# Attention scores of four heads as one group of twelve matmuls, and the side work of each unit placed anew over three fixed banks

## What is computed

```
Xp = X Wp[h] + bp        (512 x 32 for each of 8 heads)
Xc = Xp C[h]^T
S  = Xc Xp^T             (512 x 512)
attn = tanh(A * S)
out = relu(attn Xp)
```

## Time and profile before

| | before |
|---|---|
| runs (3), us | 2223.23, 2228.31, 2232.1 |
| median, us | 2228.31 |
| span of the profiled execution, us | 2229.1 |
| instructions | 38475 |
| busy: PE, PEld | 2052.3 (92%), 1499.7 (67%) |
| busy: DVE, ACT, POOL | 1538.2 (69%), 1246.9 (56%), 1062.8 (48%) |

### The profile page before, as it was taken

How to read it: one execution, slowest core, us unless ns; L and a number is a source line. 1 busy time by engine, 2 the same in 40 slices (tenths; PEclk the granted TensorE clock), 3 DMA queues, 4 the chain that set the end, 5 groups by cost and what they waited for, 6 DMA issues and landing times. The chain is left out here.

```text
span 2229.1 us, 38475 instructions
## 1 busy us (share of the span) xinstructions
PE 2052.3 (92%) x12194; PEld 1499.7 (67%) x12194; DVE 1538.2 (69%) x3332; ACT 1246.9 (56%) x1870; POOL 1062.8 (48%) x1266
## 2 busy tenths in 40 slices
PE   7999999956999999967999999999999789999986
PEld 6988888845888888853454544444444478888853
DVE  6777777744666666654687778887876557767759
ACT  4444444414666666645766766675666257767630
POOL 3355555552333333326345565464642447777740
PEclk9999999977999999987999999998998899999998
DMA  7344445125555555643122211223221055556559
GB/s 288 146 170 172 171 171 181 39 82 172 167 184 175 176 183 172 179 152 132 57 95 83 98 62 62 77 82 103 74 67 32 6 181 182 187 167 191 187 204 350
DMA packets 138148, 315.42 MB, mean 142 GB/s; under 512 B 36990, under 2 KB 67808, under 8 KB 133952
## 3 DMA queue, kind: packets, MB, share of 16 engines
q1 hardware_dynamic: 106560, 271.77, 36.3%
q0 software_dynamic: 31488, 42.39, 5.5%
HBM read 206.67 MB, written 151.56 MB: 161 GB/s over the span
## 5 line engine op out<-in xcount | busy, mean ns | idle before, releaser
L1712 ACT ACTIVATE c_att<-c_att 128x1024 f32<-128x1024 f32 x256 | 270.0, 1057 | 210.5 <-DVE c_att L1914 208.3
L1914 DVE TENSOR_TENSOR c_att<-c_p_s,adj 128x1024 f32<-128x1024 f32 x256 | 301.1, 1216 | 86.5 <-PE c_p_o L1421 74.4
L2241 POOL DMA_INDIRECT moe_y<-d_y,d_goal x256 | 257.0, 1004 | 115.9 <-ACT d_y L2206 51.5
L995 POOL DMA_INDIRECT moe_y<-b_y,b_goal x144 | 155.4, 1079 | 327.8 <-DVE b_y L1047 293.9
L1408 PEld LDWEIGHTS c_p_s<-c_xcth,c_xpth 32*128 32x128 f32 x512 | 48.0, 185 | 208.3 <-issue 121.2
L154 PE MATMUL b_p_y<-b_w2h,b_hh 128*128 128x256 f32 x576 | 169.2, 294 | 7.4 <-DVE b_hl L160 4.0
L476 POOL DMA_INDIRECT moe_in<-a_xn,a_rows x128 | 141.5, 1106 | 57.6 <-issue 29.2
L160 DVE TENSOR_TENSOR b_hl<-b_ht,b_hh 128x512 fp32r<-128x512 f32 (+1 forms) x160 | 101.5, 638 | 88.8 <-ACT b_ht L1153 88.8
L155 PE MATMUL b_p_y<-b_w2l,b_hh 128*128 128x256 f32 x576 | 160.7, 279 | 0.0
L156 PE MATMUL b_p_y<-b_w2h,b_hl 128*128 128x256 f32 x576 | 160.6, 279 | 0.0
L1364 POOL DMA_INDIRECT moe_in<-c_xn,c_rows x128 | 130.6, 1020 | 53.8 <-issue 39.4
(11 more groups left out here) (273 smaller groups left out, 6147.4 us busy)
## 6 DMA issues: line engine op xcount, KB each, us to landing
b_w<-in_moe_w SPq DMA_DIRECT2D x80, 512.0 KB, 4.3
moe_in<-b_zeros SPq DMA_DIRECT2D x65, 520.0 KB, 10.8
d_xin<-moe_in SPq DMA_DIRECT2D x64, 520.0 KB, 3.5
adj<-in_adj SPq DMA_DIRECT2D x32, 1024.0 KB, 5.6
b_xin<-moe_in SPq DMA_DIRECT2D x32, 520.0 KB, 5.9
c_g<-moe_y SPq DMA_DIRECT2D x32, 512.0 KB
moe_y<-c_zeros SPq DMA_DIRECT2D x32, 512.0 KB
d_w<-in_moe_w SPq DMA_DIRECT2D x64, 256.0 KB
```

What stands on the lines that cost most here:

```text
L995: pool.indirect_dma_start(out=m["moe0_y"], out_offset=bass.IndirectOffsetOnAxis(ap=goal[:, h, t:t + 1], axis=0), in_=y[:, h, t, :], in_off ...
L1712: act.activation(part, part, ACT.Tanh).then_inc(att_ready, 1)
L1914: dve.tensor_tensor(att[:, u % 2, 2 * c:2 * c + 2, :], p_s[:, 2 * c:2 * c + 2, :], adj[:, h, u % T, :].unsqueeze(1).broadcast_to([P, 2, N] ...
L2241: pool.indirect_dma_start(out=m["moe1_y"], out_offset=bass.IndirectOffsetOnAxis(ap=goal[:, h, t:t + 1], axis=0), in_=y[:, h, t, :], in_off ...
```

## The change

The halves of a unit's scores are merged: `scores` now issues twelve matmuls, for each of the three operand pairs four heads one after the other, and raises `s_done` once for a unit. PE waits until both products of the unit before are done. `side_a(u)` is almost empty, and the order of a unit on PE is scores(u), `side_a(u)`, values(u - 1), `side_b(u)`. PE's loop no longer reaches into the next graph: the first scores of a graph are made in its own unit 0. DVE waits once for a unit's scores, before its first product.

The three banks of `p_w` no longer swap: LEFT, RIGHT and COUNT are 0, 1 and 2, and every piece of side work has one of them. Pieces are moved: the second half of the product with C and the last transpose back of a graph now stand in its own units 0 and 1 instead of the units 5 to 7 of the graph before; `apply1` moves from unit 0 to unit 7 of the graph before; the second half of the projection is cut in two (`only`); `down` moves half a unit to a unit later; on POOL `add_moe0` goes ahead of `scale3`, and `scale1` between the two halves of the scatter. ACT runs both tanhs of a unit first and all side work behind them. The number of matmuls, activations and DVE instructions of a graph stays the same, but that the second half of the projection is issued in two calls.

The core of the diff. In PE's `side_a` and `side_b` and in DVE's `side` the removed lines, which can be read in the kernel above, are left out, and ACT's side work, which follows PE's (each bank is emptied in the unit in which PE fills it), is left out whole:

```diff
                     weigh_moe0(b + 2)
+                    add_moe0(b + 2)
                 if not is_at(b, 0):
                     scale3(b - 1)
-                if more:
-                    add_moe0(b + 2)
-                if not (isinstance(b, int) and b < 2):
+                if b > 1:
                     scatter(q - 1, h, b - 2, 0)
-                    scatter(q - 1, h, b - 2, 1)
                 if more:
                     scale1(b + 2)
+                if b > 1:
+                    scatter(q - 1, h, b - 2, 1)
...
-            def scores(b, par, u, c):
+            def scores(par, u):

                 f, t = u // T, u % T
                 s, tok = of(f, par), slice(t * P, (t + 1) * P)
                 for n, (left, right) in enumerate(((xpth, xcth), (xpth, xctl), (xptl, xcth))):
-                    for i in (2 * c, 2 * c + 1):
+                    for i in range(HG):
                         r = slice(DH * i, DH * i + DH)
                         mm = pe.matmul(p_s[:, i, :], left[r, s, tok], right[r, f, :], start=(n == 0), stop=(n == 2))
                 mm.then_inc(s_done, 1)
...
-            def wide(w, f, src, bank, done, last_of=False):
-
-                for k in range(KD):
+            def wide(w, f, src, bank, done, last_of=False, only=range(KD)):
+
+                for k in only:
                     mm = pe.matmul(p_s[:, bank, :] if last_of else p_w[:, bank, :], w[:, k, f * P:(f + 1) * P], src[:, k, :],
                                    start=(k == 0), stop=(k == KD - 1))
-                mm.then_inc(done, 1)
+                if KD - 1 in only:
+                    mm.then_inc(done, 1)
...
                def side_a(u):
+                    if u == 4 and not last:
+                        wide(wp, 1, xt, LEFT, xpt_done, only=(1,))
+                def side_b(u):
+                    if u == 0:
+                        if going_down:
+                            wide(ws3, 1, xt3, RIGHT, up_done)
+                        elif late:
+                            keep_busy(RIGHT)
+                        if late:
+                            pe.wait_ge(member_ready, b - 1)
+                            if going_down:
+                                pe.wait_ge(hs_ready, KHS * (b - 2) + 1)
+                            else:
+                                pe.wait_ge(xp_ready, GRP * b + 1)
+                            count_before(pe, m, count, member, count_done)
+                        pe.wait_ge(xpt_ready, GRP * b + 2)
+                        pe.wait_ge(xpt_lo, GRP * b + 2)
                         if going_down:
                             pe.wait_ge(sh_ready, KHS * (b - 2) + 2)
+                        elif late:
+                            pe.wait_ge(sg_ready, b - 1)
+                        project_c(h, 1, LEFT)
+                    if u == 1:
+                        if post:
+                            pe.wait_ge(ot_ready, GRP * b)
+                            if late:
+                                pe.wait_ge(r2_step, R2 * (b - 2) + 2)
+                            else:
+                                pe.wait_ge(xp_ready, GRP * b + 1)
+                            turn_back(ot[:, 1], COUNT, back_done)
+                        if going_down:
+                            pe.wait_ge(hs_ready, KHS * (b - 2) + 2)
+                            down(0, RIGHT)
+                        elif late:
+                            keep_busy(RIGHT)
+                        pe.wait_ge(xct_lo, GRP * b + 2)
+                        turn_back(xpf[:, 1], LEFT, xp_done)
+                    if u == 2:
+                        if not last:
+                            pe.wait_ge(xn_ready, b + 2)
+                            if post:
+                                pe.wait_ge(x3_ready, GRP * b)
+                            else:
+                                pe.wait_ge(xp_ready, GRP * b + 1)
+                            turn(xn, 0, COUNT, tr_done)
                             pe.wait_ge(xp_ready, GRP * b + 2)
+                            turn(xn, 1, LEFT, tr_done)
                         if going_down:
                             pe.wait_ge(x4_ready, TB * (b - 2) + 1)
+                            down(1, RIGHT)
+                    if u == 3 and not last:
+                        pe.wait_ge(xt_ready, KD * (b + 2))
+                        wide(wp, 0, xt, COUNT, xpt_done)
+                        wide(wp, 1, xt, LEFT, xpt_done, only=(0,))
+                    if u == 4:
                         if post:
+                            pe.wait_ge(xn3_ready, b)
+                            if going_down:
+                                pe.wait_ge(x4_ready, TB * (b - 1))
+                            turn(xn3[:, 1 - h], 0, RIGHT, tr3_done)
+                            if not last:
+                                pe.wait_ge(xpt_ready, GRP * (b + 1) + 1)
+                            else:
+                                pe.wait_ge(x3_ready, GRP * b)
+                            turn(xn3[:, 1 - h], 1, COUNT, tr3_done)
+                    if u == 5:
+                        pe.wait_ge(ot_ready, GRP * b + 1)
+                        if post:
+                            pe.wait_ge(xt3_ready, KD * (b - 1) + 1)
+                        turn_back(ot[:, 0], RIGHT, back_done)
+                        if not last:
+                            pe.wait_ge(xpt_ready, GRP * (b + 1) + 1)
+                            if post:
+                                pe.wait_ge(xt3_ready, KD * b)
+                            turn_back(xpf[:, 0], COUNT, xp_done)
                         if post:
                             pe.wait_ge(xt3_ready, KD * b)
+                            if not last:
+                                pe.wait_ge(xpt_ready, GRP * (b + 1) + 2)
+                            else:
+                                pe.wait_ge(xp_ready, GRP * b + 2)
+                            logits(xt3, LEFT)
+                    if u == 6:
                         if not last:
+                            pe.wait_ge(x3_ready, GRP * b + 1)
+                            pe.wait_ge(xpt_lo, GRP * (b + 1) + 1)
+                            project_c(1 - h, 0, RIGHT)
                         if going_up:
+                            pe.wait_ge(sg_ready, b)
+                            wide(ws1, 0, xt3, LEFT, up_done)
+                            pe.wait_ge(xp_ready, GRP * (b + 1) + 1)
+                            wide(ws3, 0, xt3, COUNT, up_done, only=(0,))
                         elif post:
                             pe.wait_ge(sg_ready, b)
+                            keep_busy(LEFT)
+                    if u == 7:
+                        if going_up:
+                            wide(ws3, 0, xt3, COUNT, up_done, only=(1,))
+                            pe.wait_ge(sh_ready, KHS * (b - 1) + 1)
+                            wide(ws1, 1, xt3, LEFT, up_done)
+                        elif post:
+                            keep_busy(LEFT)
+                            keep_busy(LEFT)
                 for u in range(UNITS):
-                    for c in range(2):
-                        pe.wait_ge(prod_ready, 2 * (UNITS * b + u) + c + 1)
-                        if u + 1 < UNITS:
-                            if u + 1 == T and c == 0:
-                                pe.wait_ge(xct_lo, GRP * b + 2)
-                            scores(b, h, u + 1, c)
-                        elif not last:
-                            scores(b + 1, 1 - h, 0, c)
-                        if c == 0:
-                            side_a(u)
-                            if u > 0:
-                                values(b, h, u - 1)
-                            elif post:
-                                values(b - 1, 1 - h, UNITS - 1)
-                        else:
-                            side_b(u)
+                    if post or u > 0:
+                        pe.wait_ge(prod_ready, 2 * (UNITS * b + u))
+                    if u % T == 0:
+                        pe.wait_ge(xct_lo, GRP * b + u // T + 1)
+                    scores(h, u)
+                    side_a(u)
+                    if u > 0:
+                        values(b, h, u - 1)
+                    elif post:
+                        values(b - 1, 1 - h, UNITS - 1)
+                    side_b(u)
...
             def products(b, h, u, c):
                 n = UNITS * b + u
-                if c == 0 and not (isinstance(n, int) and n < 2):
-                    dve.wait_ge(av_done, n - 1)
-                dve.wait_ge(s_done, 2 * n + c + 1)
+                if c == 0:
+                    if n > 1:
+                        dve.wait_ge(av_done, n - 1)
+                    dve.wait_ge(s_done, n + 1)
...
                 def side(u):
                     if u == 0:
                         if going_down:
+                            gate_shared(b - 2, 1, p_w[:, RIGHT, :])
                         if late:
                             places_of(b - 2)
+                        if not post:
```

(21 more changed lines are left out.)

240 lines of the change are left out of this document (59 added, 181 removed).

## The result

The changed kernel takes **2106.42 us** (median of four, 2106.05 to 2108.89); the kernel before took 2230.20 beside it. The ratio is **0.9447 [0.9423, 0.9471]**: 5.5% faster. The direction was forecast and the size was not: 124 us less instead of 80, and the time lies under the range's low end of 2118.

What follows compares the result with a forecast made beforehand. PE was taken to bound the kernel, busy 92% of the span. Savings of 38 us (graphs 2 to 8), 23 (10 to 14) and smaller terms made 80, from 2229.1 to 2149, median 2148; range 2118 to 2182.

Steps and rivals of the forecast that it cites:

- the group at 0.89 us: PE's twelve merged score matmuls of a unit run all side by side in 0.89 us, saving 7.1 us a graph.
- Rival 1: Four row strips on PE share more: 1.1 us a group, 2160 (chance 0.14), or 1.6, 2195 (chance 0.06).
- the replay: Unit-by-unit sum of PE's and DVE's work in the attention stage: 40.6 us for graphs 2 to 8, 36.7 for 10 to 14.
- New unit 3: the 4.16 of the old unit 2 less 0.60, 3.56: DVE's side work in unit 3, taken from old durations: 3.56 us, beside 2.26 for the products.
- small gaps that the replay has not; I add them: 0.8 us beyond PE's busy time added to each graph's sum, giving 41.4 and 37.5 us.
- Half-clock stretches are kept as they are.: The time PE runs at half clock in the stage was assumed unchanged.
- rival 3: PE's clock falls at gaps in late graphs: single falls 2174 (chance 0.11), a lasting one 2298 (chance 0.05).
- The small terms of the sum: Savings estimated outside the main graphs: graph 9 5 us, graphs 1, 15 and 0 6, 4 and 2, ahead of graph 0 2.
- Rival 2: DVE stands idle during every unit's scores: 1.7 us saved in seven graphs, nothing later, 2216 us; chance 0.07.
- under 35: Sign of a right forecast: DVE's waits for PE in the stage shrink from 74 us to under 35.
- Rival 4: The twelve score matmuls run one by one on PE and nothing is left of the gain; no chance of its own given.
- POOL's "thin" slack: POOL's moved steps cost nothing: about 33 us of work under 41 a graph, some 2 us to spare at scale3.

Runs made afterwards that it cites:

- e11_before_add_early: The kernel before with only POOL's add_moe0 moved ahead of scale3: 2219.31 us, ratio 0.9970.
- e6_before_busy5: The kernel before with one more keep_busy in unit 5 of graphs 9 to 15: 2221.50 us, ratio 0.9966.
- e4_merge_only: The kernel before with its scores merged and everything else in its old place: 2287.61 us, ratio 1.0242.
- e9_pool_adds: The changed kernel with nine more 128x256 additions on POOL per graph from 2 on, ahead of the scatter: ratio 0.9568 to the kernel before, on another chip.
- e1_two_by_two: The changed kernel with a unit's twelve score matmuls issued as two groups of six, still one hand-over to DVE: 2107.66 us, ratio 0.9437.

## Why the prediction was wrong in size, step by step

**Right: the group at 0.89 us.** It took 0.90, with 0.34 and 0.23 between passes, as two strips took 0.89. Rival 1 is out at both its prices, and so is what stood beside it by the Trainium skill, "TensorE: Matmul & The Clock Gate", section "Measured speedup vs the span model": at 3.07x a group would take 1.1. (In rival 1, "39.6 to 40" for the late graphs does not follow from its own rule, which gives 40.0 - 1.4 = 38.6; its 2195 is off by some 6 us.) Of the argument one sentence was false: "No row shows four row strips at once". The score rows at 1023.39 do; I had read only graph 3's, and the doubt with rival 1's 0.20 was not needed.

**Right: the replay as a method.** Its units against those of graph 5 after:

| unit | 0 | 1 | 2 | 3 | 4 | 5 | 6 | 7 |
|---|---|---|---|---|---|---|---|---|
| forecast | 5.0 | 6.13 | 4.25 | 5.82 | 4.80 | 4.1 | 5.6 | 4.94 |
| measured | 4.49 | 6.11 | 4.25 | 4.11 | 4.71 | 4.31 | 5.40 | 5.17 |

Units 1 and 2 hit to 0.02 us, 4, 5, 6 and 7 to 0.25. The forecast was 40.6 without small gaps; the units measured sum to 38.5, and unit 3 alone makes 1.7 of the difference. That is also what the two experiments with the merge say: a unit is as long as the longer of PE and DVE in it. Which of the two holds a unit came out otherwise, though. The replay gave five of eight to DVE; in graph 4 PE is busy throughout in six, all but 2 and 5, and in units 1, 4 and 7 DVE lies 0.3 us or less behind it.

**Wrong, the first step: "New unit 3: the 4.16 of the old unit 2 less 0.60, 3.56."** The duration came from a stretch in which POOL's adds blocked half of the operations, and the change moves those adds away: `add_moe0` was looked at for what waits for it, and priced at "nothing". Freed of it, the piece takes 1.4 us and unit 3 is PE's, at 4.11. That is 7 x 1.7 = 12 us in graphs 2 to 8, and, at 4.71 for 5.82, 5 x 1.1 = 5.5 in graphs 10 to 14. It is also most of the way from DVE's forecast "37" of busy time to the 34.6 measured. `e11_before_add_early` shows the cause.

**Wrong, the second: "small gaps that the replay has not; I add them".** Graph 4 has 0.45 us of idle PE, and pieces of one form side by side cost less than their rows before (a `turn_back` with another behind it takes 0.49 instead of 0.59: the rows at 1496.64 and 1497.13 below). The 0.8 should not have been added to a sum of start-to-start distances, which hold their gaps already. Some 10 us in 13 graphs.

**Wrong, the third: "Half-clock stretches are kept as they are."** They fell from 51.2 to 10.2 us; at 0.47 lost per us that is 19 us. In graphs 10, 13 and 14 of the kernel before the falls hung on the gap that `e6_before_busy5` filled (9.6 us of the 19). After the change unit 5 has `logits` behind its transposes in place of that gap, but the gap that the forecast's rival 3 foresaw, "about 1.4 us ahead of scores(3), just behind transposes", is there: it is in the first two of these rows, of graph 12.

```profile
1483.46 1.09 PE L1429 MATMUL c_p_w<-consts,c_xn 128*128 128x128 f32 x8
1485.88 0.50 PE L1409 MATMUL c_p_s<-c_xcth,c_xpth 32*128 32x512 f32 x4 [1.32 <-DVE c_att L1906]
...
1496.64 0.66 PE L1435 MATMUL c_p_w<-consts,c_ot 128*128 128x128 f32 x4
1497.13 0.60 PE L1435 MATMUL c_p_w<-consts,c_xpf 128*128 128x128 f32 x4
1497.85 1.97 PE L1454 MATMUL c_p_w<-c_wg,c_xt 128*128 128x64 f32 x16
1499.75 0.50 PE L1409 MATMUL c_p_s<-c_xcth,c_xpth 32*128 32x512 f32 x4
```

That gap stands in each of the graphs 10 to 14, 1.32 or 1.33 us long, and a second one of 1.36 to 1.39 us ahead of the next graph's first scores in graphs 10 to 13, and the granted clock stayed at 1.0 in all five graphs. So rival 3 had its gap and its fall did not follow: what failed is the reading that such a gap brings one. Why the clock held is not shown. Graph 0 had the most half clock, 17.1 us, and has 3.4; its cause was not tried.

Together 17.5 + 10 + 19 = 46.5 us, against 46 missed in the stage (123.9 measured, 78 forecast for it). That the two agree so closely is partly luck: graphs 2 to 8 were missed by 20 us, where the first two steps give 18, and graph 0 by 4, where its clock gives 6. The small terms of the sum lie within 3 us of what was measured but for graph 0 (5.8 instead of 2, by its clock).

**Rival 2** (the hand-over exposed in each unit, 2216) did not come in the changed kernel, because the placement gives DVE work in every unit. But DVE's wait of 55.5 us is above the "under 35" that was to show the forecast right: in units where PE is the slower side DVE waits at the scores, and unit 3, lost to PE, is one more of these (0.45 us in graph 4). PE's waits at the scores, which were to grow, fell from 26.2 to 18.4 us, because PE and not DVE is the bound. `e4_merge_only` came out worse than that rival, at 2288, by another way: the ring over the two buffers of `att`. **The chances**: faster at 0.89 was sound; the range's low end took in gaps and one clock loss (2118) but no duration that the change itself would shorten.

**Rival 4** is out: the rows say x4, and the time went. **POOL's "thin" slack** held: its scaling steps still wait 74.8 us for DVE in the stage. It ends where `e9_pool_adds` puts 6.6 us a graph on POOL.

## What to carry to other kernels

Before a duration of a small operation goes into a sum, look at what other engines did in that moment: ten DVE operations of 4 to 8 elements took 3.6 us beside POOL's adds and 1.4 without, and a change that moves POOL's work moves DVE's durations. When two engines' half-steps are merged into one hand-over per step, each step lasts as long as its slower side, so the side work must be balanced step by step: the merge alone made this kernel 2.4% slower, and with the placement 5.5% faster. In a ring of three engines, ask which buffer closes it; PE running ahead costs time where the work it runs ahead of frees that buffer.

## What the hardware showed that was not expected

- Twelve matmuls on four row strips ran four at a time whatever the order of issue (`e1_two_by_two`: 0.33 and 0.24 us between passes, as interleaved).
- A DVE operation of 0.17 us on 4 elements took 0.62 when an add of POOL had begun 0.02 us before it (`e9_pool_adds`, a TENSOR_SCALAR). In the kernel before a COPY, with one input like it, took 0.66 and a TENSOR_TENSOR 0.73.
- PE's clock fell behind an idle stretch of 1.43 us after short transposes, and stayed up with one `keep_busy` in that place. But the changed kernel has idle stretches of 1.3 and 1.4 us in each late graph, the first behind short transposes too, and its clock stays at 1.0; without any `keep_busy`, PE idle for 7 of 36 us a graph, the mean clock of the stage was still 0.97. The length of a gap alone does not tell whether the clock falls.
